# Global attention: a second, negated table of row scales, and a plain multiplication for the exponential's bias

## The chip, the core and the metric

One Trainium2 chip, one of its cores. The kernel is one launch. The metric is the device time of a launch in microseconds; the time before is the median of 3 runs.

## What is computed

The input `x` has 8 sequences of 512 tokens with 128 values each, all in f32. It is normalized per token, and two branches are added to it:

- **Global attention**, 16 heads of 64, on all 512 tokens of a sequence. Queries and keys are scaled to unit length, the products are multiplied by one scale per head, and a softmax over 512 keys follows:

```python
qn = q / jnp.maximum(jnp.linalg.norm(q, axis=-1, keepdims=True), EPS)
kn = k / jnp.maximum(jnp.linalg.norm(k, axis=-1, keepdims=True), EPS)
scale = jnp.exp(jnp.minimum(logit_scale, MAX_LOG_SCALE))
cos_dots = jnp.einsum('bhid,bhjd->bhij', qn, kn) * scale
attn = jax.nn.softmax(cos_dots, axis=-1)
```

- **Six layers** of local attention (windows of 32, rotary tables, a mask) and a gated feed-forward net.

The change touches the global attention only.

## The kernel before

The program runs its stages one after the other: a short setup with the statistics of all tokens, global attention, then six layers, then the output. Each engine has its own program, and the order on each engine is written out by hand; semaphores tie the engines together.

**Global attention.** The work is cut into periods. A period `a` is one pair of heads of one sequence, so there are 8 sequences by 8 pairs, 64 periods. A period has four steps `j`, one for each block of 128 queries (256 steps in all). The function `periods` yields them, and `all_batches` runs the first and the last sequence written out and the six between in a loop. The stages of a pair overlap: while pair `i` is in its exponentials, pair `i + 2` is projected, the lengths of pair `i + 1` are worked out, and the output of pairs `i - 1` and `i - 2` is made.

One step `j` of pair `i`, by lines of the kernel:

- TensorE multiplies queries by keys (L960) into two PSUM banks, 512 columns for each of the two heads.
- VectorE takes each row's largest product, two numbers in each partition (`amx`, L716), and multiplies it by minus the row's scale (`anm`, L721).
- ScalarE takes the exponential of `scale * product + bias` with `srn` as scale and `anm` as bias, once for each head, and sums the row into `aden` (L537).
- VectorE takes the reciprocal of the sums (`ardn`, L712). GpSimd multiplies the 1024 exponentials of each partition by it (L441).
- TensorE transposes the result in two halves of four blocks, head 0 (L972) and head 1 (L1019). ScalarE copies the first half out of PSUM (L517), VectorE the second (L732). Both halves use one bank, so the second may start when the first has been copied.

Once in a period, other work sits between these steps. VectorE at `j == 2`, behind its copy L732: the table `srn` for the next pair (L739: 8 numbers in each partition, reciprocal length by head scale), and the keys times their reciprocal lengths (L742). VectorE at `j == 3`: the keys' copy (L726), the sums of squares of the pair after that (L747), two operations for a floor and a first guess of the reciprocal root (L749, L751). GpSimd then does 12 small steps of Newton's method (L326 of the helper `newton`), four each ahead of its multiplications L441 at `j` 0, 1 and 2. At `j == 0` VectorE adds an output block to the result (L703). TensorE has projections (L1032, L1002), transposes of queries and keys (L996, L1013), the product with the values (L984) and the output product (L1043) in between.

Before the global attention VectorE caps the logits (L652), sets some rows (L654 to L657), waits until ScalarE has taken the exponential of the 16 head scales in place in `sc` (semaphore `s_sc` at 2), and goes on to the statistics (L665).

The lines that the change touches are L739 to L740 (the table `srn`), L720 to L722 (the bias `anm`), the declarations near L103 and L114, and the setup at L658.

Of the kernel before, what the change touches and what calls it, by code (L numbers as in the profile page):

```python
# [12 lines left out]
P = 128  # L13
ALU = mybir.AluOpType
# [7 lines left out]
H, DH = 16, 64  # L22
# [6 lines left out]
NU = SEQ // P  # L29
# [15 lines left out]
def build(nc, x_in, consts, a_logit, a_bout, a_wqk, a_wv, a_wo, l_wqk, l_wv, l_wo, l_scale, l_w1, l_w2, l_small, out):  # L45
# [7 lines left out]
    with ExitStack() as ctx:  # L53
        def sb(name, shape, dt=F32):
            return ctx.enter_context(nc.sbuf_tensor(name, shape, dt))
# [3 lines left out]
        def sem(name, credit=0):  # L59

            s = ctx.enter_context(nc.semaphore(name))
            credits[name] = (s, credit)
            return s
# [37 lines left out]
        den = sb("den", [P, H])  # L101
        rden = sb("rden", [P, H])
        sc = sb("sc", [P, H])  # L103
        boutb = sb("boutb", [P, DIM])
        st = sb("st", [P, NU, 6])
        agg = sb("agg", [P, NU, 2])
# [5 lines left out]
        arn = sb("arn", [P, NU * 4])  # L112
        art = sb("art", [P, NU * 4])
        srn = sb("srn", [P, 2, NU, 2])  # L114
        amx = sb("amx", [P, NU, 2])
        anm = sb("anm", [P, NU, 2])
        aden = sb("aden", [P, NU, 2])
# [30 lines left out]
        def bank(n, w=1):  # L148
            return ps[:, 512 * n:512 * (n + w)]
# [15 lines left out]
        s_sc = sem("s_sc")  # L165
# [33 lines left out]
        a_nm = sem("a_nm")  # L199
# [92 lines left out]
        def periods(b, first, last):  # L292

            for a in range(-2 if first else 0, PAIRS + 3 if last else PAIRS):
                yield a, b * PAIRS + a, lambda d, a=a: (not first or a + d >= 0) and (not last or a + d < PAIRS)
# [8 lines left out]
        def past(eng, s, n):  # L306

            if not (isinstance(n, int) and n <= 0):
                eng.wait_ge(s, n)
# [5 lines left out]
        def heads(ap, n):  # L315
            return ap.rearrange("p (h d) -> p h d", h=n)
# [328 lines left out]
        def _(dve):  # L645
# [10 lines left out]
            dve.wait_ge(s_row, 1)  # L656
            nc.vector.memset(fh[ONES_ROW:ONES_ROW + 1, :, NC - 1], 1.0).then_inc(s_row, 1)  # L657
            dve.wait_ge(s_sc, 2)  # L658


            with dve.Fori(0, NB) as b:
# [16 lines left out]
            def normalize_tokens(b):  # L678

                tokens = acc[:, bass.ds(b * SEQ, SEQ)]  # L680
                dve.wait_ge(a_xcp, at("a_xcp", b))
                past(dve, a_xt, b)
                nc.vector.tensor_tensor(heads(xnn, NU), heads(tokens, NU),
                                        mv[:, bass.ds(b * NU, NU), 0:1].to_broadcast([P, NU, DIM]), ALU.subtract).then_inc(a_dev, 1)
                dve.wait_ge(a_dev, b + 1)
                nc.vector.tensor_tensor(heads(xnn, NU), heads(xnn, NU),
                                        rstd[:, bass.ds(b * NU, NU)].unsqueeze(2).to_broadcast([P, NU, DIM]),
                                        ALU.mult).then_inc(a_xn, 1)
                nc.vector.tensor_tensor(heads(tokens, NU), heads(tokens, NU), boutb[:].unsqueeze(1).to_broadcast([P, NU, DIM]),
                                        ALU.add).then_inc(a_b, 1)  # L690

            def attend(b, first, last):
                for a, i, has in periods(b, first, last):
                    for j in range(NU):
                        if j == 0 and has(-3):
                            n = i - 3
                            tokens = acc[:, bass.ds((b - (a < 3)) * SEQ, SEQ)]
                            dve.wait_ge(a_o, n + 1)
                            if (a - 3) % PAIRS == 0:
                                dve.wait_ge(a_b, b + (a >= 3))  # L700
                            else:
                                dve.wait_ge(a_acc, n)
                            nc.vector.tensor_tensor(tokens, tokens, ps_b, ALU.add).then_inc(a_acc, 1)  # L703
                        if j == 2 and has(-2):
                            n = i - 2
                            dve.wait_ge(a_y, n + 1)
                            past(dve, a_o, n - 1)
                            nc.vector.tensor_copy(oTA[:, a % 2], ps_y).then_inc(a_ysb, 1)
                        if has(0 if j else -1):
                            t, v = i * NU + j - 1, (j - 1) % NU  # L710
                            dve.wait_ge(a_e, t + 1)
                            nc.vector.reciprocal(ardn[:, v], aden[:, v]).then_inc(a_rd, 1)  # L712
                        if has(0):
                            t = i * NU + j
                            dve.wait_ge(a_s, t + 1)
                            nc.vector.tensor_reduce(amx[:, j], bank(j % 2 * 2, 2).rearrange("p (s k) -> p s k", s=2), X,  # L716
                                                    ALU.max).then_inc(a_mx, 1)
                            dve.wait_ge(a_mx, t + 1)
                            if j == 0:
                                dve.wait_ge(a_sr, i + 1)  # L720
                            nc.vector.scalar_tensor_tensor(out=anm[:, j], in0=amx[:, j], scalar=-1.0, in1=srn[:, a % 2, j],  # L721
                                                           op0=ALU.mult, op1=ALU.mult).then_inc(a_nm, 1)  # L722
                        if j == 3 and has(1):
                            n = i + 1
                            dve.wait_ge(a_tk, n + 1)
                            nc.vector.tensor_copy(kTA[:, (a + 1) % 2], ps_a).then_inc(a_kT, 1)  # L726
                        if has(-1 if j < 2 else 0):
                            n, v = i * NU + j - 2, (j - 2) % NU
                            dve.wait_ge(a_pt1, n + 1)
                            if v == 0:  # L730
                                past(dve, a_y, i - 1)
                            nc.vector.tensor_copy(pTA[:, (a - (j < 2)) % 2, 1, :, v * P:(v + 1) * P],  # L732
                                                  ps_pt.rearrange("p (k q) -> p k q", k=NU)).then_inc(a_pT1, 1)
                        if j == 2 and has(1):
                            n, v = i + 1, (a + 1) % 2
                            c = (a + 1) % PAIRS
                            root = arn[:].rearrange("p (u c) -> p u c", u=NU)
                            dve.wait_ge(a_rs, (n + 1) * RS_POOL)
                            nc.vector.tensor_tensor(srn[:, v], root[:, :, 0:2], sc[:, 2 * c:2 * c + 2].unsqueeze(1)  # L739
                                                    .to_broadcast([P, NU, 2]), ALU.mult).then_inc(a_sr, 1)  # L740
                            keysA = qkA[:, v, :, P:2 * P].rearrange("p u (h d) -> p u h d", h=2)
                            nc.vector.tensor_tensor(keysA, keysA, root[:, :, 2:4].unsqueeze(3).to_broadcast([P, NU, 2, DH]),  # L742
                                                    ALU.mult).then_inc(a_kn, 1)
                        if j == 3 and has(2):
                            n = i + 2
                            dve.wait_ge(a_sq, 2 * n + 2)
                            nc.vector.tensor_reduce(ass[:], heads(sqA, NU * 4), X, ALU.add).then_inc(a_ss, 1)  # L747
                            dve.wait_ge(a_ss, n + 1)
                            nc.vector.tensor_scalar(ass[:], ass[:], NORM_FLOOR, 0.5, ALU.max, ALU.mult).then_inc(a_fl, 1)  # L749
                            dve.wait_ge(a_fl, n + 1)  # L750
                            nc.vector.tensor_scalar(arn[:].bitcast(I32), ass[:].bitcast(I32), -0.5,  # L751
                                                    float(0x5F3759DF - (1 << 22)), ALU.mult, ALU.add).then_inc(a_gs, 1)
                        if a == 4 and j == 1 and not last:
                            normalize_tokens(b + 1)

            normalize_tokens(0)
            all_batches(dve, attend)


# [522 lines left out]
```

## Time and profile before

| | |
|---|---|
| median of 3 runs | 5019.32 us (5016.16 to 5022.33) |
| the profiled execution | 5020.55 us |
| its span, first to last instruction | 5018.7 us |
| TensorE busy | 4554.7 us, 91% of the span |
| VectorE busy | 4077.1 us, 81% |
| ScalarE busy | 3003.4 us, 60% |
| GpSimd busy | 2491.4 us, 50% |
| `anm` (L721) on the chain that ended last | 3% of the span |
| `amx` (L716) on that chain | 3% of the span |

The global attention lies between about 50 and 1236 us of the span. The other stages fill the rest. The table's shares are averages over all stages. "Busy" counts the time between an instruction's recorded start and end; the record of an instruction that waits inside for something includes that wait. TensorE is PE, VectorE is DVE, ScalarE is ACT and GpSimd is POOL in the rows.

### The profile page before, as it was taken

The page shows a single profiled execution, that of the slowest core. Times are in us where ns is not written, and L with a number is a line of the kernel's source. Part 1 is how long each engine was busy: PE and PEld are TensorE (multiplying, and loading weights), DVE is VectorE, ACT ScalarE, POOL GpSimd, SP SyncE. Part 2 cuts the span into 40 slices and gives each one's busy share as a digit, 9 for nine tenths or more (in the row PEclk, how much of TensorE's full clock was granted, in tenths as well). Part 3 has the DMA queues.
Part 4 walks back from the last instruction along what each step waited for, and adds up shares of the span by engine and source line. Part 5 has one row for each costly group of instructions (what it writes and reads, how often), then busy time and mean ns, then how long its engine had stood idle before and what let it go on. Part 6 is the DMA issues. An engine that isn't in the chain of part 4 may idle for free.

```text
span 5018.7 us, 103927 instructions
## 1 busy us (share of the span) xinstructions
PE 4554.7 (91%) x37352; PEld 3155.9 (63%) x37352; DVE 4077.1 (81%) x5941; ACT 3003.4 (60%) x4796; POOL 2491.4 (50%) x3919
## 2 busy tenths in 40 slices
PE   5999999998899988999889998899988999889997
PEld 3555555554677756777567775677756777567775
DVE  6888888886899958998589985899958999589995
ACT  4666666665666636666366663666636666366663
POOL 3555555554566605666056660566605666056660
PEclk9999999999999999999999998999989999899998
DMA  1000000000000000000000000000000000000001
GB/s 46 1 1 0 0 0 0 0 1 17 1 0 0 20 21 1 0 0 21 19 1 0 0 21 19 1 0 0 21 20 1 0 0 21 20 3 2 0 1 30
DMA packets 65826, 39.11 MB, mean 8 GB/s; under 512 B 52000, under 2 KB 61984, under 8 KB 64672
## 3 DMA queue, kind: packets, MB, share of 16 engines
q1 hardware_dynamic: 65568, 35.97, 2.5%
q8 instruction: 125, 2.05, 0.2%
q14 instruction: 133, 1.09, 0.1%
HBM read 21.30 MB, written 2.10 MB: 5 GB/s over the span
## 4 chain that ended last, share of the span: by engine, by line
POOL 34%; issue 28%; PE 16%; DVE 15%; ACT 4%; POOLq 2%; DVEq 0%; DMA 0%; SPq 0%; ACTq 0%
POOL t L468 9%; POOL rt L326 9%; POOL t L458 7%; POOL pn L463 6%; DVE amx L716 3%; DVE anm L721 3%; POOL rn L326 3%; PE ps L1168 3%; PE ps L1157 2%; ACT t L537 2%; DVE ass L747 1%; PE ps L1069 1%; POOLq L325 1%; PE ps L984 1%; PE ps L1002 1%
## 5 line engine op out<-in xcount | busy, mean ns | idle before, releaser
L458 POOL TENSOR_TENSOR t<-t 128x1024 f32<-128x1024 f32 x192 | 453.2, 2361 | 1503.2 <-DVE t L782 1503.2
L1069 PE MATMUL ps<-mh,y 128*128 128x128 f32 x6144 | 741.4, 280 | 116.3 <-ACT qT L565 90.8
L1069 PEld LDWEIGHTS ps<-mh,y 128*128 128x128 f32 x6144 | 711.2, 194 | 157.5 <-issue 157.5
L927 PE MATMUL ps<-wqk,xsT 128*128 128x512 f32 x1536 | 734.8, 622 | 13.3 <-ACT xsT L590 13.3
L441 POOL TENSOR_TENSOR t<-t,ardn 128x1024 f32<-128x1024 f32 x256 | 484.6, 1893 | 299.5 <-DVE ardn L712 299.5
L537 ACT ACTIVATE t<-ps,anm,srn 128x512 f32<-128x512 f32 x512 | 392.8, 771 | 273.1 <-DVE anm L721 273.1
L577 ACT ACTIVATE pT<-ps 128x1024 f32<-128x1024 f32 x192 | 196.8, 1025 | 591.6 <-PE ps L1079 591.6
L927 PEld LDWEIGHTS ps<-wqk,xsT 128*128 128x128 f32 x1536 | 285.3, 196 | 365.5 <-issue 345.6
L780 DVE TENSOR_TENSOR t<-ps,tabl 128x1024 f32<-128x1024 f32 x384 | 461.9, 1203 | 63.4 <-ACT sq L607 57.4
L828 DVE TENSOR_TENSOR qn<-t,rn 128x2048 f32<-128x2048 f32 x192 | 440.1, 2292 | 65.4 <-POOL rn L326 65.3
L782 DVE TENSOR_TENSOR t<-ps,tabl 128x512 f32<-128x512 f32 x768 | 491.1, 681 | 0.0
L551 ACT ACTIVATE y<-ps 128x1024 f32<-128x1024 f32 x384 | 372.1, 1021 | 176.9 <-PE ps L1142 176.9
L468 POOL TENSOR_TENSOR t<-t 128x1024 f32<-128x1024 f32 x192 | 455.2, 2371 | 0.4 <-DVE t L782 0.2
L933 PEld LDWEIGHTS ps<-cst,qn 128*128 128x128 f32 x3072 | 359.4, 144 | 152.3 <-DVE qn L828 93.1
L801 DVE TENSOR_REDUCE ss<-sq 128x32 f32<-128x2048 f32 x192 | 437.0, 2276 | 0.0
L933 PE MATMUL ps<-cst,qn 128*128 128x128 f32 x3072 | 382.3, 279 | 48.0 <-DVE qn L828 48.0
L463 POOL TENSOR_TENSOR pn<-es,rden 128x1024 f32<-128x1024 f32 x192 | 365.6, 1904 | 105.1 <-DVE rden L794 105.1
L817 DVE TENSOR_REDUCE mx<-ps 128x16 f32<-128x1024 f32 x192 | 235.2, 1225 | 218.7 <-PE ps L1106 218.7
L1142 PE MATMUL ps<-pT,xw 64*128 64x256 f32 x3072 | 383.5, 389 | 6.7 <-ACT pT L577 6.7
L1106 PE MATMUL ps<-kpad,qT 128*32 128x128 f32 x12288 | 378.2, 275 | 0.0
L1106 PEld LDWEIGHTS ps<-kpad,qT 128*32 128x32 f32 x12288 | 326.2, 110 | 44.9 <-issue 44.6
L1142 PEld LDWEIGHTS ps<-pT,xw 64*128 64x128 f32 x3072 | 280.9, 186 | 57.6 <-ACT pT L577 8.1
(134 smaller groups left out, 8633.1 us busy)
## 6 DMA issues: line engine op xcount, KB each, us to landing
wqk<-in_l_wqk SPq DMA_DIRECT2D x6, 1024.0 KB, 5.0
xsh<-x SPq DMA_DIRECT2D x48, 128.0 KB
xsh<-x SPq DMA_DIRECT2D x48, 127.0 KB
wv<-in_l_wv SPq DMA_DIRECT2D x6, 512.0 KB, 5.7
wo<-in_l_wo SPq DMA_DIRECT2D x6, 512.0 KB, 6.7
acc<-in_x_in SPq DMA_DIRECT2D x8, 256.0 KB, 5.8
out_dram<-x SPq DMA_DIRECT2D x8, 256.0 KB, 2.4
w<-in_l_w SPq DMA_DIRECT2D x6, 341.0 KB, 3.1
```

What stands on the lines that cost most here:

```text
L326: nc.gpsimd.tensor_tensor(to, a, b, op).then_inc(done, 1)
L441: nc.gpsimd.tensor_tensor(eA[:, v], eA[:, v], ardn[:, v].unsqueeze(2).to_broadcast([P, 2, SEQ]), ALU.mult).then_inc(a_pn, 1)
L458: nc.gpsimd.tensor_tensor(t1[:, 0:INNER], t1[:, 0:INNER], t2[:, 0:INNER], ALU.add).then_inc(l_rotq, 1)
L463: nc.gpsimd.tensor_tensor(heads(pn[:], H), heads(es[:], H), rden[:].unsqueeze(2).to_broadcast([P, H, KEYS]), ALU.mult).then_inc(l_p, 1)
L468: nc.gpsimd.tensor_tensor(t1[:, INNER:2 * INNER], t1[:, INNER:2 * INNER], t2[:, INNER:2 * INNER], ALU.add).then_inc(l_rotk, 1)
L537: e = act.activation(eA[:, j, h], bank(j % 2 * 2 + h), ACT.Exp, bias=anm[:, j, h:h + 1], scale=srn[:, a % 2, j, h:h + 1], accum_out=aden[: ...
L782: sine = nc.vector.tensor_tensor(t23[:, :, lo:lo + DH // 2], q3[:, :, hi:hi + DH // 2], tabl[:, 1, u, i, lo:lo + DH // 2].unsqueeze(1).to_ ...
L927: m = nc.tensor.matmul(pool[:, s * 512:(s + 1) * 512], src, wqk[:, i * INNER + s * 512:i * INNER + (s + 1) * 512], start=True, stop=True)
L933: t = nc.tensor.transpose(pool[:, a * P:(a + 1) * P], src[:, i * INNER + a * P:i * INNER + (a + 1) * P], ident)
L1069: m = nc.tensor.matmul(ps_o, y[:, h], mh[:, slot(h)], start=(h == 0), stop=(h == H - 1))
L1106: m = nc.tensor.matmul(pool1[w * WIN:(w + 1) * WIN, a * 2 * KEYS:(a + 1) * 2 * KEYS], qT[:, a, w * WIN:(w + 1) * WIN], kpad[:, 2 * a:2 * a ...
L1142: m = nc.tensor.matmul(pools[odd][:, w * PAIRS * WIN:(w + 1) * PAIRS * WIN], xw[rows, n % NU, w], pT[rows, :, w * WIN:(w + 1) * WIN], star ...
```

## The change

`nsc` is minus `sc`, made once in the setup; `nsrn` is minus `srn`, made once a period behind it; `anm` becomes a multiplication of `amx` by `nsrn` in place of an operation with two multiplications.

```diff
+        nsc = sb("nsc", [P, H])
...
+        nsrn = sb("nsrn", [P, 2, NU, 2])
...
             dve.wait_ge(s_sc, 2)
+            nc.vector.tensor_scalar(nsc[:], sc[:], -1.0, None, ALU.mult).then_inc(s_sc, 1)
+            dve.wait_ge(s_sc, 3)
...
                             if j == 0:
                                 dve.wait_ge(a_sr, i + 1)
-                            nc.vector.scalar_tensor_tensor(out=anm[:, j], in0=amx[:, j], scalar=-1.0, in1=srn[:, a % 2, j],
-                                                           op0=ALU.mult, op1=ALU.mult).then_inc(a_nm, 1)
+                            nc.vector.tensor_tensor(anm[:, j], amx[:, j], nsrn[:, a % 2, j], ALU.mult).then_inc(a_nm, 1)
...
                             nc.vector.tensor_tensor(srn[:, v], root[:, :, 0:2], sc[:, 2 * c:2 * c + 2].unsqueeze(1)
+                                                    .to_broadcast([P, NU, 2]), ALU.mult)
+                            nc.vector.tensor_tensor(nsrn[:, v], root[:, :, 0:2], nsc[:, 2 * c:2 * c + 2].unsqueeze(1)
                                                     .to_broadcast([P, NU, 2]), ALU.mult).then_inc(a_sr, 1)
```

The semaphore `a_sr` is now raised by the second of the two tables.

## Rows read from the trace of the kernel before

**Rows 1.** Busy time by engine in the steady part of the global attention.
```profile
100.00:1200.00 1100.00, 1049.90 (x5779) 565.58 (x5777) 920.37 (x1460) 709.54 (x1564) 609.79 (x967) 1.00 0.00 1
```
**Rows 2.** Waits, 100 to 1200 us: us in total, times, longest us.
```profile
ACT t L537 <- DVE anm L721: 249.7, 187, 2.8
...
PE ps L1019 <- ACT kpad L517: 41.8, 60, 0.9
```
**Rows 3.** The chain that ended last, 500 to 540 us: start us, us, what.
```profile
506.18 0.16 DVE srn L739
...
524.42 0.15 DVE srn L739
```
**Rows 4.** Timeline, 500 to 520 us, all engines: start us, us, engine, line.
```profile
505.58 0.69 DVE L732 COPY kpad<-ps 128x512 f32<-128x512 f32 x1 [1.14 <-PE ps L1019]
506.18 0.16 DVE L739 TENSOR_TENSOR srn<-arn,sc 128x8 f32<-128x8 f32 x1
506.26 0.69 DVE L742 TENSOR_TENSOR qn<-qn,arn 128x512 f32<-128x512 f32 x1
...
506.86 0.16 DVE L712 RECIPROCAL ardn<-aden 128x2 f32<-128x2 f32 x1
...
507.10 1.89 POOL L441 TENSOR_TENSOR t<-t,ardn 128x1024 f32<-128x1024 f32 x1 [2.67 <-DVE ardn L712]
...
508.12 0.66 PE L1013 MATMUL ps<-cst,qn 128*128 128x128 f32 x4
508.18 0.83 DVE L721 SCALAR_TENSOR_TENSOR anm<-amx,srn 128x2 f32<-128x2 f32 x1
...
511.37 0.17 DVE L749 TENSOR_SCALAR ass<-ass 128x16 f32<-128x16 f32 x1
511.58 0.17 DVE L751 TENSOR_SCALAR arn<-ass 128x16 int32<-128x16 int32 x1
...
511.83 0.21 POOL L326 TENSOR_TENSOR art<-arn 128x16 f32<-128x16 f32 x1 [2.84 <-DVE arn L751]
...
512.26 0.16 DVE L712 RECIPROCAL ardn<-aden 128x2 f32<-128x2 f32 x1
...
512.90 1.89 POOL L441 TENSOR_TENSOR t<-t,ardn 128x1024 f32<-128x1024 f32 x1
...
513.58 1.24 DVE L721 SCALAR_TENSOR_TENSOR anm<-amx,srn 128x2 f32<-128x2 f32 x1
...
514.92 0.78 ACT L537 ACTIVATE t<-ps,anm,srn 128x512 f32<-128x512 f32 x1 [2.54 <-DVE anm L721]
...
517.41 0.61 ACT L517 ACTIVATE kpad<-ps 128x512 f32<-128x512 f32 x1
...
518.07 0.66 PE L1019 MATMUL ps<-cst,t 128*128 128x128 f32 x4 [0.76 <-ACT kpad L517]
```
**Rows 5.** Instructions that touch `srn`: duration ns min/median/max, first and last start.
```profile
L721 DVE SCALAR_TENSOR_TENSOR anm<-amx,srn x256: 163/833/1840, 56.6 to 1220.1; 128x2 f32<-128x2 f32 x128
L739 DVE TENSOR_TENSOR srn<-arn,sc x64: 151/158/168, 51.7 to 1202.2; 128x8 f32<-128x8 f32 x64
```
**Rows 6.** VectorE groups, 35.9 to 38.1 us (setup): busy us, mean ns, idle.
```profile
L343 DVE SCALAR_TENSOR_TENSOR artmp<-rstd 128x32 f32<-128x32 f32 x3 | 0.6, 192 | 0.1
L344 DVE TENSOR_TENSOR artmp<-artmp,av 128x32 f32<-128x32 f32 x3 | 0.6, 191 | 0.1
```
**Rows 7.** Timelines of VectorE and of GpSimd, 1005 to 1032 us.
```profile
1015.58 0.68 DVE L683 TENSOR_TENSOR pn<-acc,mv 128x512 f32 x1
...
1015.78 0.56 POOL L326 TENSOR_TENSOR arn<-arn,art 128x16 f32<-128x16 f32 x1
```
**Rows 8.** Timeline of VectorE, 0 to 58 us: the setup.
```profile
19.33 0.91 DVE L657 MEMSET fh<- 1x1024 f32 x1 [0.27 <-DVE fh L655]
20.27 0.87 DVE L665 BATCH_NORM_STATS2 st<-acc 128x6 f32 x4
```

## The prediction, made before any run of the changed kernel

> **What bounds the kernel now.** I read four views in this order: busy time by stretch, the waits, the chain that ended last, and one period of the timeline. Only the global attention is touched, 1.19 ms of the run; nothing of the layers that follow is changed, so they keep their time.
>
> In its steady part TensorE is busy for 1049.90 of 1100 us [rows 1]. It has little room: one stall in each period, where the second half of a transpose (L1019) waits for ScalarE's copy L517, 41.8 us over 60 periods, or 0.70 us in each [rows 2]. So a loop through other engines sets the pace, by less than a microsecond a period. The chain shows which: it passes through the table `srn` once a period, at 506.18 and 524.42 us [rows 3], so a period takes 18.24 us and VectorE's small operation L739 lies on the loop.
>
> The timeline [rows 4] gives the loop piece by piece. TensorE ends a transpose, and VectorE's copy L732 starts at 505.58 after an idle wait. Back to back behind it come `srn` (506.18), the keys L742 (506.26) and the reciprocal (506.86). That reciprocal releases GpSimd's multiplication L441, 507.10 to 508.99. The bias `anm` starts at 508.18, needs some 0.16 us of work, its minimum [rows 5], and ends at 509.01, 0.02 us behind GpSimd. VectorE then runs its queue down to L751 at 511.58; GpSimd does four Newton steps from 511.83 and its next L441 from 512.90 to 514.79. Again `anm` starts early (513.58) and ends at 514.82, 0.03 us behind GpSimd. ScalarE, idle for 2.54 us until then, starts its exponentials at 514.92, three copies follow, the last at 517.41, and TensorE gets its bank at 518.07. From there TensorE runs through to the transpose that releases the next L732.
>
> The thing to see is `anm`: 163 ns at the least, 833 in the median, 1840 at most [rows 5], for two numbers per partition. In both places above it ends when GpSimd's multiplication does, whatever its start. Its length is a wait inside the instruction, not work. It reads two operands in SBUF while GpSimd reads SBUF too. ScalarE's 249.7 us of waiting for `anm` [rows 2] are mostly this.
>
> **The change part by part.** The sum is made against the profiled execution, 5020.55 us, which stands 1.2 us over the median of the runs, 5019.32.
>
> 1. *The form of `anm`, 256 times.* Two per period lie on the loop (508.18 and 513.58); the other two are off it, since ScalarE's and TensorE's other work covers them. The work itself: the old form and the new one side by side at 32 elements take 192 and 191 ns [rows 6]; the old form at 2 elements takes 163 at the least, the new form at 8 elements 151 to 168 [rows 5]. So the work shrinks by 1 ns, at most by 12 (163 less 151). I take 1, by the like-for-like pair: 2 x 64 x 1 ns = 0.1 us; the upper end is 1.5 us. What remains is the wait for GpSimd. The new form also reads two SBUF operands. No row shows a plain multiplication waiting for GpSimd, but one shows the reverse: L683, a plain subtraction of two SBUF operands, ran from 1015.58 to 1016.26, and a Newton step begun at 1015.78 took 0.56 us, ending 0.08 us behind it [rows 7], where such a step takes 0.21 in the ordinary period [rows 4]. So the plain two-operand form meets GpSimd at the same place, and I take the wait as unchanged: 0. The other end, the wait gone, is the first rival.
>
> 2. *The table `nsrn`, 64 times.* It has the shape and form of `srn`, 158 ns in the median [rows 5]. What counts is how much later the next instruction starts. `srn` starts at 506.18 and L742 at 506.26, so a small operation with no wait behind it moves its follower by 0.08 us, half its duration [rows 4]. The nearest rows for the other end: L749 to L751, where a wait on a semaphore stands between, 0.21 us [rows 4]. The low end is 0, if some slack on the loop takes it. `nsrn` has no wait on either side, like `srn` ahead of L742, so I take 0.08. Does it stay on the loop? L742, the reciprocal, GpSimd's L441, `anm`, VectorE's queue to L751, the Newton steps, L441 and `anm` again all start when the one before them allows, and the stall of TensorE at the end says that the loop is the later party. TensorE's transpose of the keys, L1013 at 508.12, needs L742, which ends at 506.95 [rows 4]: 1.1 us to spare. GpSimd stands idle for 2.67 us before 507.10 [rows 4], so `nsrn` does not meet it and cannot be held up by it. Cost: 64 x 0.08 = 5.1 us. TensorE's stall grows from 0.70 to 0.78 us. The last two periods, where fewer stages run, may hide theirs (0.2 us, left in the sum).
>
> The Trainium skill ("VectorE: DVE Perf Modes", the section on the DRAIN that can't be avoided) says that the next operation doesn't start until the pipe of the one before has emptied, and that the number of operations is what to save. Taken alone it speaks against this change and prices `nsrn` at its whole duration; the same page lets an operation that is not held start earlier, and the row above sides with that. The whole-duration price is the second rival.
>
> 3. *`a_sr` raised by `nsrn`.* Its waiter is the first `anm` of the next period, over 7 us later (506.26 against 513.58) [rows 4]. Cost 0, with that cover.
>
> 4. *The setup.* One operation of 16 elements and a wait for it, on VectorE between L657 and L665 [rows 8]. TensorE waits for what VectorE makes there, so it counts in full. Priced like L749 to L751, 0.21 us.
>
> 5. *Nothing else.* No DMA, no queue of SyncE or GpSimd is touched. The two tiles are 64 bytes per partition each.
>
> Sum: -0.1 + 5.1 + 0 + 0.2 = +5.2 us. 5020.55 + 5.2 = 5025.75 for the profiled execution, and from the median, 5019.32 + 5.2 = 5024.5. That is 0.10%; a measurement of this kernel can tell about 0.2% (10 us) from no change.
>
> **The rivals.**
>
> *First, the plain form doesn't wait for GpSimd.* Then `anm` takes 0.16 us, ScalarE's exponentials at 514.92 move forward by up to 1.1 us, and the stall of TensorE goes. TensorE then paces the stage, so the gain is capped by its stall: 0.70 x 64 = 45 us [rows 2], and `nsrn` is hidden in what is left: 5019.3 - 45 = 4974. For it: no row has the new form start while L441 runs. Against it: [rows 7], and that the two forms have the same operands. The Trainium skill ("SBUF — State Buffer", the section on its two sides) has a VectorE operation with two SBUF inputs and a GpSimd operation that reads SBUF exclude each other for the whole of the instruction that started first, whatever the form; by that rule this rival is void, and no run here has shown it for the plain form yet. Chance 6%.
>
> *Second, slower: `nsrn` costs its whole duration on the loop.* The place is VectorE's queue between 506.18 and 506.86. At 158 ns the price is 64 x 0.158 = 10.1, with the setup 10.3 us, so 5029.6; at 0.21 us, as behind a semaphore, 13.6 us and 5032.9. It decides from 0.157 us a period on, where the sum passes 10 us. For it: the page's rule above. Against it: two operations of the same kind in the same place start 0.08 us apart. Chance 7%.
>
> *Third, slack takes it.* Some piece of the loop has slack that the rows don't show, or the plain form saves its full 12 ns twice a period: 0 to +3 us, 5019.5 to 5022. This is still no measurable change. Chance 17%.
>
> **How the numbers follow.** The forecast itself (between +3 and +9 us) has 69%, the third rival 17%, the second 7%, the first 6%, and 1% is for a gain of another kind. No change within 0.2%: 69 + 17 less 1 that runs over, 85%. Slower: 7 + 1 = 8%. Faster: 6 + 1 = 7%. The range: the low end is the unchanged time less the 3 us by which the runs shown scatter, 5016.3, rounded to 5016; the high end takes in the whole-duration price of 5029.6 and rounds up to 5031. The first rival and the second's upper price stay outside.
>
> **What would show it right or wrong.** In the changed kernel's profile: `anm` as a plain multiplication still with a median near 0.8 us, its ends within 0.03 us of the ends of L441; L742 starting 0.16 us behind `srn` instead of 0.08; a period of 18.32 us; TensorE's stall before L1019 near 0.78 us. If `anm` has a median near 0.16 us and the stall is gone, the first rival holds. If `srn` and L742 start 0.24 us or more apart, the second does. If the period is 18.24 us with `nsrn` in place, the third does. The layers' stretch should be equal in both; a difference there would be something that I haven't seen.

## The result and the profile after

The changed kernel takes 5038.18 us (median of 6 runs, 5024.76 to 5043.65) against 5020.82 for the kernel before (6 runs). The ratio is 1.0035, with a 95% interval from 1.0019 to 1.0050: slower, by 10 to 25 us. The forecast was 5024.5 with a range up to 5031. The profiled execution took 5037.21 us, its span is 5035.4 us.

**The bias.** The instructions that read or write `anm`, from the changed kernel's trace (duration ns min/median/max, first and last start):

```profile
L725 DVE TENSOR_TENSOR anm<-amx,nsrn x256: 160/832/1836, 58.0 to 1241.6; 128x2 f32<-128x2 f32 x128
```

The old form had 163/833/1840 [rows 5]. The plain form waits as long. The 1 to 4 ns by which it looks shorter don't belong to the form: the old form beside the two tables shows them too (experiment 3).

**The added table.** VectorE's timeline of the changed kernel (start us, us, engine, line):

```profile
535.72 0.15 DVE L742 TENSOR_TENSOR srn<-arn,sc 128x8 f32<-128x8 f32 x1
535.80 0.16 DVE L744 TENSOR_TENSOR nsrn<-arn,nsc 128x8 f32<-128x8 f32 x1
535.87 0.68 DVE L747 TENSOR_TENSOR qn<-qn,arn 128x512 f32<-128x512 f32 x1
```

L747 starts 0.15 us behind `srn`, where it was 0.08 [rows 4]. The chain that ended last, changed kernel, 520 to 580 us:

```profile
535.72 0.15 DVE srn L742
...
554.02 0.16 DVE srn L742
...
572.32 0.16 DVE srn L742
```

A period takes 18.30 us. Before, two intervals in a row (524.42 to 542.65 to 560.88) took 18.23 us each, and the one of [rows 3] 18.24. So the table costs 0.065 us a period and 64 x 0.065 = 4.2 us. TensorE's stall ahead of L1024 (L1019 before) is 43.8 us over 58 times, 0.755 us each, where 0.70 stood before and 0.78 was forecast. Up to here the forecast's terms held, and they leave 13 us to be found.

**What was not forecast.** The waits of VectorE in the attention, 100 to 1240 us, first before, then after (us in total, times, longest):

```profile
DVE acc L703 <- issue: 3.1, 6, 0.6
```
```profile
DVE acc L707 <- issue: 15.9, 6, 3.3
```

L703 and L707 are one statement, the first of a sequence's first period. "issue" is time in which the engine waited for nothing that the profile shows. Six starts are the six passes of the loop over the middle sequences: one entry and five backward branches. The third of them in both traces, first before:

```profile
493.09 0.17 DVE L751 TENSOR_SCALAR arn<-ass 128x16 int32<-128x16 int32 x1
493.83 0.69 DVE L703 TENSOR_TENSOR acc<-acc,ps 128x512 f32 x1 [0.56 <-issue]
```
```profile
500.40 0.18 DVE L756 TENSOR_SCALAR arn<-ass 128x16 int32<-128x16 int32 x1
503.63 0.69 DVE L707 TENSOR_TENSOR acc<-acc,ps 128x512 f32 x1 [3.05 <-issue]
```

The loop's entry costs 0.25 us (202.86 us, the same view). What is new is about 2.6 us at each backward branch, 15.9 - 3.1 = 12.8 us in all. It stands on the loop that sets the pace: the chain of the kernel before passes L703 at 493.83 us, at this branch, and at 511.66 in the period behind it. The queues that bring instructions tell what the engine waited for. The page's lines on DMA queues (packets, MB, share), before and after:

```profile
q8 instruction: 125, 2.05, 0.2%
q14 instruction: 133, 1.09, 0.1%
```
```profile
q8 instruction: 134, 2.20, 0.2%
q14 instruction: 158, 1.29, 0.1%
```

25 more packets of 8 KB on q14: five for each of five branches. The changed program fetches code again at every branch that the program before had at hand. The trace has the start of each packet. In the third pass of the changed kernel, set beside the same pass before, the five added ones start at 502.1, 503.9, 524.3, 586.4 and 647.2 us: one while VectorE waits at the branch, one as it starts again, the others as it works through the loop, with 130 and 129 VectorE instructions recorded between the last three.

TensorE shows a wait of the same kind, once. Its timeline in the changed kernel:

```profile
502.45 2.08 PE L965 MATMUL ps<-qk 64*128 64x512 f32 x4 [3.59 <-issue]
```

It comes with nine more packets of 16 KB on q8, the first of them at 497.7, 498.7 and 502.8 us. TensorE's instructions were not changed.

By stage: GpSimd's first fill after the attention starts at 1236.14 us before and 1257.71 after, 21.6 us later. Where they went can be read sequence by sequence. The table has the time from `srn` in the first period of one sequence to `srn` in the first period of the next, in us, for these two kernels and four of the experiments below. The five backward branches lie in columns 3 to 7, one in each; TensorE's wait, where there is one, lies in column 4.

| kernel | 1 | 2 | 3 | 4 | 5 | 6 | 7 |
|---|---|---|---|---|---|---|---|
| before | 141.84 | 146.91 | 147.24 | 147.17 | 147.18 | 147.17 | 147.17 |
| after | 144.61 | 147.48 | 150.49 | 151.66 | 150.25 | 150.39 | 150.23 |
| after, moved by 64 (2) | 142.53 | 147.47 | 147.81 | 152.46 | 147.72 | 147.70 | 147.71 |
| before, moved by 10 (5) | 144.71 | 146.92 | 149.94 | 149.67 | 149.66 | 149.88 | 149.69 |
| before, moved by 20 (1) | 144.67 | 146.88 | 149.75 | 152.21 | 149.88 | 149.70 | 149.63 |
| before, moved by 80 (6) | 142.05 | 146.96 | 147.25 | 151.07 | 147.17 | 147.16 | 147.17 |

- Column 2 has neither a backward branch nor a wait of TensorE: 0.57 us for the tables of eight periods, some 4.4 in all.
- Columns 3, 5, 6 and 7 lose another 2.6 us each: 12.9 for five branches.
- TensorE's wait (498.86 to 502.45 us) overlaps VectorE's (500.58 to 503.63), and column 4 is only 1.3 us above its neighbours.
- Column 1, ahead of the loop, loses 2.2 us more than its tables explain. From 78 to 82 us the granted clock of TensorE was 0.61 in the changed kernel, so part of that time went by at the lower of its two levels (1.2 and 2.4 GHz), and 1.00 before. Why it fell there is open.
- The setup and the way to the first `srn` take 0.65 us more, 0.55 of them at the statistics (L669 starts at 20.82 us, where L665 started at 20.27 [rows 8]).

That makes 21.4 of 21.6 us. The rest of the span, unchanged work, took 4.9 us less. Its length varies by such amounts from one execution to the next (last section).

### The profile page after: what moved, and what is told of

Read it like the earlier page. It is cut to its first block, busy times and chain, and to the rows that moved or that the text cites. A ratio compares the mean times of both kernels' runs of the same rounds, so it can differ in the third digit from the quotient of the medians.

```text
span 5035.4 us, 103992 instructions
## 1 busy us (share of the span) xinstructions
PE 4552.8 (90%) x37352; PEld 3156.0 (63%) x37352; DVE 4077.6 (81%) x6006; ACT 3001.1 (60%) x4796; POOL 2491.2 (49%) x3919
## 4 chain that ended last, share of the span: by engine, by line
POOL 34%; issue 29%; PE 16%; DVE 15%; ACT 4%; POOLq 2%; DVEq 0%; DMA 0%; SPq 0%; ACTq 0%
POOL t L470 9%; POOL rt L328 8%; POOL t L460 7%; POOL pn L465 7%; DVE amx L720 3%; POOL rn L328 3%; DVE anm L725 3%; PE ps L1173 3%; PE ps L1162 2%; ACT t L539 1%; DVE ass L752 1%; PE ps L989 1%; POOLq L327 1%; PE ps L1007 1%; PE ps L965 1%
```

## The experiments

Two theories stood. **Code**: most of the loss is code fetched at the loop's branch, because the loop's place in VectorE's program and its length changed. **Periods**: the loss is the added operation, 0.25 us in each of 64 periods.

All fills below are one-column fills of an unused tile on VectorE, ahead of the attention's loop in a stretch where VectorE stood idle for 6.4 us. "Start" and "length" count VectorE's instructions in the built program.

**1. The kernel before, moved by 20.**

```diff
             normalize_tokens(0)
+            for k in range(20):
+                nc.vector.memset(junk[:, k:k + 1], 0.0)
             all_batches(dve, attend)
```

> The kernel before with 20 one-column fills of an unused tile on VectorE, placed ahead of the attention loop where VectorE stood idle for 6.4 us; the loop itself is unchanged. Code theory: the 16 to 17 us come mostly from VectorE's loop of the six middle sequences, whose backward branch now waits about 3 us for code, because the loop sits elsewhere in the program and is longer. A mere shift of 20 instructions should then bring the same wait to the kernel before: L703's idle time put down to issue goes from 3.1 to about 16 us over 6 starts, and the time rises by 11 to 15 us. Rival, cost of the periods: the 16 us are 0.25 us in each of 64 periods, from the added table. Then this kernel takes the time of before within 2 us.

5039.58 us, ratio 1.0038 [1.0024, 1.0051]. No table, no new form, and the loss is that of the change. Its waits:

```profile
DVE acc L704 <- issue: 16.0, 6, 3.2
```

Its queues moved 134 packets on q8 and 158 on q14, as after the change. That settles the main cause: the place of the loop is enough. The time rose by 19 us, over the 11 to 15 expected. The attention alone ends 18.2 us later (1254.38 us): some 12.7 at the branches, 2.8 in the first sequence, and 2.5 by a wait of TensorE like the one in the changed kernel (3.4 us long, partly beside VectorE's own).

**2. The changed kernel, moved by 64** (the same edit with 64).

> The changed kernel with 64 such fills in the same idle stretch. Code theory: the shift by 64 instructions moves the loop to a place where it is held whole; the issue idle ahead of L707 falls from 15.9 to about 3 us, and the kernel runs 10 to 14 us faster than the changed one, 3 to 7 us slower than before. Rival, cost of the periods: as the changed kernel, 16 us slower than before.

5033.27 us, ratio 1.0025 [1.0016, 1.0034], 4.9 us faster than the changed kernel by the medians and 12.7 slower than before, where 10 to 14 and 3 to 7 were expected. Of the profile the expectation held, of the time only half:

```profile
DVE acc L708 <- issue: 3.0, 6, 0.6
```

q14 is back at 134 packets. The attention ends at 1245.92 us, 11.8 us earlier than in the changed kernel. By the table above the branches' 12.9 us are gone, and the 2.1 us of the first sequence too, but TensorE's wait (3.2 us here) has nothing left beside it and costs 4.7 us in place of 1.3. Behind the attention this profiled execution was 7.8 us longer than the changed kernel's, at a mean granted clock of 0.974 against 0.977 (last section), so the medians give back less.

**3. Both tables, old form.**

```diff
-nc.vector.tensor_tensor(anm[:, j], amx[:, j], nsrn[:, a % 2, j], ALU.mult).then_inc(a_nm, 1)
+nc.vector.scalar_tensor_tensor(out=anm[:, j], in0=amx[:, j], scalar=-1.0, in1=srn[:, a % 2, j],
+                               op0=ALU.mult, op1=ALU.mult).then_inc(a_nm, 1)
```

> The changed kernel with both tables, but the bias still made in the old form with two multiplications (the negated table is made and not read). Both the code theory and the cost of the periods say: the form of the instruction doesn't matter, so the time is that of the changed kernel, 15 to 18 us slower than before, anm median 833 ns. If the plain form itself costs time, through the meeting with GpSimd or otherwise, this kernel is nearer to before.

5039.46 us, ratio 1.0039 [1.0026, 1.0053]; `anm` 160/832/1837 ns, issue idle 16.5 us, a period of 18.30 us. As the changed kernel in each of them: the form does nothing, to the time, to the wait or to the period.

**4. Both tables by one operation.**

```diff
-nc.vector.tensor_tensor(srn[:, v], root[:, :, 0:2], sc[...] ..., ALU.mult)
-nc.vector.tensor_tensor(nsrn[:, v], root[:, :, 0:2], nsc[...] ..., ALU.mult).then_inc(a_sr, 1)
+nc.vector.tensor_tensor(srns[:, :, v], root[:, :, 0:2].unsqueeze(1).to_broadcast([P, 2, NU, 2]),
+                        scs[:, :, 2 * c:2 * c + 2].unsqueeze(2).to_broadcast([P, 2, NU, 2]),
+                        ALU.mult).then_inc(a_sr, 1)
```

> The plain form of the bias, with both tables written by one operation of 16 elements (srn and its negative in one tile), so the loop has as many instructions as before and sits one instruction later. Code theory: no added wait at the branch, no added period cost but some 8 ns; before plus 0.5 to 1.5 us. Rival, cost of the periods through the added operation: also about before. A third theory, that the plain form is what costs: as the changed kernel, 16 us slower than before.

5022.55 us, ratio 1.0005 [0.9996, 1.0014], issue idle 3.1 us. The change's idea without its added instructions costs nothing that the medians can tell, and brings nothing.

**5. The kernel before, moved by 10** (the edit of experiment 1 with 10).

> The kernel before with 10 fills, the distance by which the change moved the start of the loop, the loop itself unchanged at 310 instructions (the changed kernel's has 318). If the move alone carries the loop over a border of the code's blocks: issue idle of L703 near 16 us, time near 5037. If it takes the eight added instructions as well: issue idle near 3 us, time of before within 2 us. The code theory leaves both open; this settles which part of the change did it.

5033.41 us, ratio 1.0024 [1.0013, 1.0035], issue idle 16.0 us, 158 packets on q14. The attention ends at 1252.31 us, 16.2 later than before: 12.9 at the branches, 2.9 in the first sequence, where the granted clock fell again (0.73 from 78 to 82 us). The move of the start by ten instructions, which the change made by the tables of the first sequence (written out ahead of the loop) and by `nsc`, is enough; the eight in the loop weren't needed. q8 stays at 125 packets and TensorE's long wait is not there, so that wait is another matter.

**6. The kernel before, moved by 80** (the same with 80).

> The kernel before with 80 fills, a move eight times as far as the one of 10 that cost 13 us. The runs so far all fit code held in blocks of 128 instructions of VectorE, three of which can be branched over without a wait; by that the loop of 310 instructions is held whole again: issue idle of L703 near 3 us, and the time of before plus 0 to 5 us (the upper end if TensorE waits once for its own code, 3.2 to 3.6 us, as it did in four kernels). Rival, any move away from the old place costs: 16 us of idle and 5033 to 5040 us.

5021.54 us, ratio 0.9999 [0.9990, 1.0008]:

```profile
DVE acc L704 <- issue: 3.0, 6, 0.6
```

Moved eight times as far, the loop is whole again. What counts is where it falls, not how far it went. TensorE waited 3.31 us once here. The median doesn't show it, the trace does: the attention ends at 1240.43 us, 4.3 later than before, 3.9 of them in the sequence with the wait (column 4).

**7. Two more copies of the table** on top of experiment 2, read by nobody.

```diff
+for extra in more:
+    nc.vector.tensor_tensor(extra[:, v], root[:, :, 0:2], nsc[...] ..., ALU.mult)
```

> The changed kernel with 64 fills and two more copies of the table nsrn made in each period, which nobody reads. Term of the forecast: a small operation with no wait behind it moves what follows by 0.08 us and all of it is on the loop, so two more add 0.16 us to each of 64 periods, 10 us over the kernel with 64 fills alone. Rival, an operation costs its whole 0.158 us: 20 us. Rival, slack on the loop takes it: under 4 us.

5038.39 us, ratio 1.0036 [1.0023, 1.0049]; 5.1 us over experiment 2 by the medians. The chain, 520 to 580 us:

```profile
536.69 0.16 DVE srn L744
...
555.16 0.15 DVE srn L744
...
573.62 0.16 DVE srn L744
```

18.465 us a period, 0.165 more for two operations, and the attention ends 11.0 us later (1256.88 us), where 10 were expected. A small operation costs half of its 0.16 us, all of it on the path: the forecast's term, measured alone. The medians, again, show only part of it.

**8. The bias without a second tensor.** The forecast's first rival said what the wait for GpSimd is worth; the plain form didn't remove it. A form with one tensor and a pointer operand might. 40 fills keep the longer loop whole.

```diff
-nc.vector.scalar_tensor_tensor(out=anm[:, j], in0=amx[:, j], scalar=-1.0, in1=srn[:, a % 2, j],
-                               op0=ALU.mult, op1=ALU.mult).then_inc(a_nm, 1)
+for h in range(2):
+    bias = nc.vector.tensor_scalar(anm[:, j, h:h + 1], amx[:, j, h:h + 1],
+                                   srn[:, a % 2, j, h:h + 1], -1.0, ALU.mult, ALU.mult)
+bias.then_inc(a_nm, 1)
```

> The kernel before, with the bias made by two VectorE operations a step, one for each head: the row's largest product times the scale read as a one-column pointer operand, times -1. No table is added. 40 fills ahead of the loop, so that its 342 instructions are held whole. Port theory: the old and the plain form wait for GpSimd since each reads two tensors in SBUF; with one tensor and a pointer there is nothing to wait for, so each operation takes 0.16 us or so, the stall of TensorE ahead of L1019 (0.70 us a period) goes, and the kernel is 35 to 48 us faster than before. Rival: any small VectorE operation waits while GpSimd multiplies; then the median of the first of the two stays near 0.8 us and the time is that of before or some 5 us over it.

4974.18 us, ratio 0.9912 [0.9896, 0.9927]: 45 us faster than the kernel before, 0.9%. The instructions that write `anm`, and a piece of its timeline:

```profile
L723 DVE TENSOR_SCALAR anm<-amx,srn x512: 201/208/216, 58.1 to 1178.4; 128x1 f32<-128x1 f32 x171
```
```profile
527.09 1.89 POOL L442 TENSOR_TENSOR t<-t,ardn 128x1024 f32<-128x1024 f32 x1 [3.23 <-DVE ardn L713]
...
528.16 0.34 DVE L723 TENSOR_SCALAR anm<-amx,srn 128x1 f32<-128x1 f32 x2
...
528.53 0.78 ACT L538 ACTIVATE t<-ps,anm,srn 128x512 f32<-128x512 f32 x1 [0.72 <-DVE anm L723]
```

GpSimd's multiplication runs until 528.98, and both operations of the bias end at 528.50. At the same place before, the single one ended with GpSimd (508.99 and 509.01 [rows 4]). No instance in 512 took over 216 ns. In the whole trace 507 of the 512 start inside an instruction of GpSimd; of the 256 old ones, before, all did, and 255 ended within 0.04 us of its end. So the wait belongs to the second tensor in SBUF, not to small operations as such, and not to the double multiplication. Each of the new operations writes one column; whether one with a pointer and two or more columns stays as free was not tried. TensorE is now busy for 1075.08 us of the 1100 that had 1049.90 [rows 1]; the last 6 us already lie behind this kernel's attention:

```profile
100.00:1200.00 1100.00, 1075.08 (x5926) 579.31 (x5924) 819.02 (x1739) 718.82 (x1590) 628.84 (x975) 1.00 0.01 3
```
```profile
PE ps L1024 <- ACT kpad L518: 1.7, 4, 0.6
```

Its stall of 41.8 us [rows 2] is down to 1.7. Twice the operations, 45 us less. The attention ends at 1194.15 us, 42.0 earlier, although TensorE now waits twice for its code (6.5 us in all), which makes the two sequences concerned 2.8 and 4.2 us longer than their neighbours. The other five lie 5.5 to 5.9 us below those before, 0.7 us a period.

**9. The same, without the 40 fills.**

> The same without the 40 fills: the loop then lies across one block of code more. Code theory: about 3 us at each of the five backward branches (the issue idle of L703 at 14 us or more), of which TensorE's slack hides some: 5 to 15 us slower than with the fills. Rival, place doesn't matter: the same time as with them.

4985.49 us, ratio 0.9929 [0.9912, 0.9947], issue idle 15.7 us, 159 packets on q14. 11 us slower than experiment 8 for 40 fills less, as much as the attention is longer (it ends at 1205.38 us): code again.

**One rule for all places.** Starts, lengths and VectorE's issue idle at L703:

| kernel | start | length | idle us |
|---|---|---|---|
| before | 262 | 310 | 3.1 |
| tables by one operation | 263 | 310 | 3.1 |
| moved by 10 | 272 | 310 | 16.0 |
| moved by 20 | 282 | 310 | 16.0 |
| moved by 80 | 342 | 310 | 3.0 |
| after; both tables, old form | 272 | 318 | 15.9; 16.5 |
| after, moved by 64 | 336 | 318 | 3.0 |
| three tables | 354 | 334 | 3.0 |
| pointer, moved by 40 | 334 | 342 | 3.0 |
| pointer | 294 | 342 | 15.7 |

A packet of q14 is 8 KB (1.09 MB / 133), and VectorE ran 130 and 129 instructions between two of them, so a block of code is taken here as 128 instructions, an estimate from these counts. If a loop that lies in three such blocks has its start at hand when it branches, and one that touches a fourth doesn't, all eleven kernels fit with one free number, the instructions that run ahead of the program's first. In that count the kernel before begins its loop at 65 to 73 of a block (the move by 10 must cross, the move by 1 must not), and three blocks hold 384: 384 - 310 - 65 leaves it at most nine instructions to spare. One thing had no part in the fit: moved by ten, the changed kernel's loop should begin at 75 to 83 and leave its first block after 45 to 53 instructions. From L707 at 503.63 us, the loop's fourth instruction, to the packet at 524.3 the trace has 45, so 48 from its start. The places alone would also fit blocks of 256 with two at hand; the packets' size, the odd number of five at each branch and the 130 and 129 instructions between them speak against that. The Trainium skill ("Runtime: NRT & Kernel Launch", the section on instruction fetch mechanics) says that prefetch runs straight ahead, and that a taken branch whose target isn't in the present window forces a fetch of the target's page before execution goes on. The traces agree: about 3.1 us at each such branch against 0.6 at the others, and five more packets with each. The same section gives blocks of 16 KiB for every engine; here q14's are 8 KB.

## Why the prediction was wrong

- **The sign and three terms were right.** The wait for GpSimd stayed (step 1: forecast 0 change, 833 to 832 ns); the shorter work that step 1 took, 0.1 us of the sum, isn't there (experiment 3). `nsrn` moves its follower by 0.08 us and all of it is on the loop (step 2: forecast 5.1 us, found 4.2 from the period; the doubled dose gave 0.0825 an operation). `a_sr` cost nothing. The form doesn't explain the 0.015 us between 0.08 and 0.065: the old form with both tables has the same period of 18.30 us (experiment 3).
- **The step that failed is the fifth, "Nothing else. No DMA, no queue of SyncE or GpSimd is touched".** Added instructions are code, and code comes by DMA. The loop's ten-place move put it across one more block, 12.8 us in five branches, 2.5 times the sum that was forecast. TensorE's wait for code, 1.3 us here, belongs to the same step. The 2.2 us of the first sequence, at a lower granted clock, were in no step, and their cause is open. The rows to ask were there: L703's idle put down to issue, once for each sequence, and the two instruction queues on the page of before. The question, "how much room has this loop in its blocks?", wasn't asked.
- **The setup was mis-sized**: 0.55 us for 0.21. The operation (`nsc`, L661) lasted 0.17 us, and the first statistics then started after 0.34 us of idle time put down to the wait for it.
- **The second rival, the whole duration, comes nearest in time and for the wrong reason.** 5032.9, its upper end, is 5.3 us below what was measured, but L747 starts 0.15 us behind `srn`, not 0.24 or more. The rule of the Trainium skill ("VectorE: DVE Perf Modes", the section on the DRAIN) taken alone was refuted by the row, twice.
- **The first rival had the mechanism's worth nearly right**: 4974 us if the wait goes. The plain form doesn't make it go, and a pointer operand does, at 4974.18. That the figures meet so closely is luck: without the wait the attention is some 49 us shorter (42.0, and 7.0 that TensorE's waits for code took back), not 45. Its rule ("SBUF — State Buffer", the section on the two sides, of the Trainium skill: two SBUF inputs against a GpSimd operation that reads SBUF) is now shown here from both ends.

## What to carry to other kernels

Before an instruction is added to an unrolled loop, or ahead of it, look at the idle time put down to issue at the loop's first instruction, and at the instruction queues' packets: if the loop nearly fills its blocks, a few instructions cost a code fetch at each branch, and a few dozen empty ones in an idle stretch ahead of it may take that away (11.8 us of attention in experiment 2, 11.2 between experiments 9 and 8). If a tiny VectorE operation lasts 0.8 us and ends with GpSimd's, count its tensors in SBUF: here a pointer operand in the place of the second one was worth two operations for one.

## What the runs showed that wasn't expected

- Three microseconds for a branch, from a move of ten instructions, and none from a move of eighty.
- TensorE's own wait of 3.2 to 3.6 us at the third pass of the loop: once in the changed kernel and in experiments 1, 2, 3, 6 and 7, twice (6.5 and 6.7 us) in both with the pointer, with nine or eighteen more 16 KB packets on q8, though its instructions are the same in all. It is missing before, with one operation for both tables, and with the move by 10: where VectorE's program is at most 10 instructions longer than before, and it is there from 20 on. What sets it is open. Where it stands alone it costs 3.9 to 4.7 us (experiments 6, 7 and 2), and 1.3 to 2.5 where VectorE waits for code beside it (the changed kernel, experiments 3 and 1).
- The first sequence, ahead of the loop, is 2 to 3 us longer in the changed kernel and in experiments 1 and 5, where the granted clock of TensorE was 0.61, 0.72 and 0.73 from 78 to 82 us; it was 1.00 before and in experiment 2. Each kernel has one trace, so whether this goes with the kernel or with the execution is open.
- Executions of one kernel differ by up to 21 us with the mean granted clock of TensorE: the changed kernel took 5043.65 us at 0.973 and 5024.76 at 0.982. Fitted over the runs of all kernels, one thousandth less goes with 1.9 us more. So the 21.6 us of the attention aren't contradicted by 17.4 between medians, but the last 4 us aren't settled, in this pair or in experiments 2 and 7. The 3 us of scatter from which the forecast took the low end of its range were those of three runs.
